# Both product blocks ahead of the fourth projection, and both mask sets ahead of the gates and norms, in the projection rounds of a decoder layer

## The reference

```
q_in = silu(causal_dwconv(x @ Wq, wq_conv))      # k_in, v_in in the same way, 4 taps
q, k = l2norm(q), l2norm(k)                      # per head, 4 heads of 32
v, kb = v * beta[..., None], k * beta[..., None] # beta = sigmoid(x @ Wb)
inv = -(kb @ swap(k)) * strict_lower             # in chunks of 32 tokens, then solved row by row
attn = q @ swap(k) * lower_incl
```

## Time and profile before

| What | us |
|---|---|
| median of 3 runs | 472.37 |
| profiled execution | 472.83 |
| its span | 471.1 |
| busy TensorE, VectorE, ScalarE, GpSimdE | 350.7, 317.4, 152.0, 37.4 |
| the three rounds and the tail | about 31 to 91.5 of the span |

### The profile page before, as it was taken

The page is one execution under the profiler, slowest core; times in us unless marked ns, Lnnn a source line. Parts: engine busy times, 40 slices in busy tenths (PEclk is TensorE's granted clock), DMA queues, the critical chain, the costliest instruction groups (busy, mean ns, idle before and its releaser), DMA issues.

```text
span 471.1 us, 8238 instructions
## 1 busy us (share of the span) xinstructions
PE 350.7 (74%) x2912; PEld 239.2 (51%) x2912; DVE 317.4 (67%) x1049; ACT 152.0 (32%) x267; POOL 37.4 (8%) x74
## 2 busy tenths in 40 slices
PE   3978985968952468343374998979989799878992
PEld 2544553768940456111243556565566555655672
DVE  3046567768999825966536957668876788777535
ACT  1232332223354335222030442224422343314240
POOL 6000000007940000000000000000000000000000
PEclk9999998579966556655567899998999989998997
DMA  7670110299625500000010000000200000000000
GB/s 215 193 196 25 22 22 0 53 287 245 179 69 115 111 4 5 0 1 0 0 46 1 22 1 0 24 0 1 68 1 22 0 0 22 0 1 1 24 1 22
DMA packets 51601, 23.54 MB, mean 50 GB/s; under 512 B 18248, under 2 KB 51056, under 8 KB 51312
## 3 DMA queue, kind: packets, MB, share of 16 engines
q1 hardware_dynamic: 35056, 14.71, 12.5%
q10 hardware_dynamic: 16512, 8.39, 7.0%
HBM read 18.77 MB, written 3.28 MB: 47 GB/s over the span
## 4 chain that ended last, share of the span: by engine, by line
DVE 40%; PE 38%; issue 12%; DMA 4%; ACT 4%; DVEq 1%; SPq 0%; ACTq 0%; POOL 0%
PE bank L484 6%; PE bank L706 5%; PE bank L714 5%; DVE prod L1458 4%; DVE inv L1460 4%; PE bank L459 3%; DVE as_t L1438 3%; DVE nt L1162 3%; DVE nt L1163 3%; PE bank L478 2%; DVE as_t L1260 2%; PE bank L511 2%; DVE as_t L1251 2%; DMA early<-blocks 2%; DVE sm L1164 2%
## 5 line engine op out<-in xcount | busy, mean ns | idle before, releaser
L714 PEld LDWEIGHTS bank<-w_sb,as_t 128*128 128x128 f32 x512 | 61.1, 194 | 22.9 <-issue 18.8
L1018 ACT ACTIVATE as_t<-bank,cb 128x512 f32<-128x512 f32 x64 | 43.3, 686 | 76.1 <-PE bank L706 60.8
L714 PE MATMUL bank<-w_sb,as_t 128*128 128x128 f32 x512 | 63.9, 280 | 5.0 <-ACT as_t L1018 5.0
L706 PE MATMUL bank<-as_t,w_sb 128*128 128x512 f32 x128 | 66.6, 648 | 0.0
L1438 DVE SCALAR_TENSOR_TENSOR as_t<-bank,as_t 128x128 f32<-128x128 f32 x128 | 36.0, 344 | 23.4 <-PE bank L714 21.1
L459 PE MATMUL bank<-ident,as_t 128*128 128x128 f32 (+1 forms) x64 | 12.1, 319 | 33.9 <-DVE as_t L1260 15.7
L484 PE MATMUL bank<-wtap,xc_pad 128*128 128x384 f32 x96 | 35.5, 509 | 0.0
L706 PEld LDWEIGHTS bank<-as_t,w_sb 128*128 128x128 f32 x128 | 24.1, 207 | 20.2 <-issue 18.8
L1229 DVE TENSOR_TENSOR as_t<-bank,masks 128x512 f32 (+1 forms) x32 | 20.0, 686 | 17.2 <-PE bank L511 17.2
L459 PE MATMUL bank<-ident,early 128*128 128x128 f32 x96 | 17.2, 309 | 17.7 <-DVE early L1208 6.0
L459 PEld LDWEIGHTS bank<-ident,as_t 128*128 128x128 f32 (+1 forms) x64 | 7.4, 145 | 42.1 <-DVE as_t L1260 17.3
(11 more groups left out here) (217 smaller groups left out, 614.1 us busy)
## 6 DMA issues: line engine op xcount, KB each, us to landing
toep<-taps_back ACTq DMA_DIRECT2D x8, 1024.0 KB, 8.6
toep<-x SPq DMA_DIRECT2D x8, 256.0 KB, 2.7
early<-x SPq DMA_DIRECT2D x4, 256.0 KB, 3.6
w_sb<-w SPq DMA_DIRECT2D x1, 1024.0 KB
w_sb<-w SPq DMA_DIRECT2D x2, 512.0 KB
blocks<-as_t SPq DMA_DIRECT2D x16, 64.0 KB, 2.0
early<-blocks SPq DMA_DIRECT2D x1, 1024.0 KB, 8.0
src<-vb SPq DMA_DIRECT2D x16, 64.0 KB, 6.5
```

What stands on the lines that cost most here:

```text
L706: pe.matmul(ps[4 + half][:, :], w1_sb[:, e, half * 128:half * 128 + 128], x2_c.rearrange("p b t -> p (b t)"), start=True, stop=True).then_ ...
L714: last = pe.matmul(bank(6 + e % 2)[:, b, :], hid[:, e % 2, half, b * L:(b + 1) * L], w2_sb[:, e, half, :], start=(half == 0), stop=(half = ...
L1018: act.activation(hid[:, e % 2, half, :], ps[4 + half][:, :], ACT.Relu, bias=c_of("b1", 2 * e + half)).then_inc(s["hid_ready"], 1)
```

## The change

In a round TensorE now issues both product blocks before the fourth projection: the order is projection 0, keys, projection 1, block 0, projection 2, block 1, projection 3. It was projection 0, keys, projection 1, projection 2, block 0, projection 3, block 1. VectorE now writes the second mask set directly after the first, before `gate_sums` and `norms`; before, it followed them. No instruction is added, removed or resized, and the tail keeps its code.

```
@@ project_step (TensorE)
                 project(g, 1)
+                products(g - 1, 0)
                 project(g, 2)
-                products(g - 1, 0)
+                products(g - 1, 1)
                 project(g, 3)
-                products(g - 1, 1)
                 if more:
                     x_transposed(g + 1)
@@ the loop over the rounds (VectorE)
                 mask_products(g - 1, 0)
+                mask_products(g - 1, 1)
                 gate_sums(g)
                 norms(g)
-                mask_products(g - 1, 1)
```

## The result

The changed kernel took 475.14 us, the median of six runs (475.02 to 477.15); the kernel before took 471.77 us, the median of six (470.93 to 473.17). The ratio is 1.0083, with a 95% interval of 1.0057 to 1.0108: slower. The forecast was 476.0 us in a range of 474.2 to 477.7.

A forecast was written before the change was run, and what follows sets the result against it. The prediction took a gapless TensorE chain of projections and block 0, then ScalarE's squares and VectorE's reduction, to bound the rounds. Rounds 3.81 + mask waits 0.15 - tail 0.30 = 3.66 us gave 476.0 us, range 474.2 to 477.7.

The forecast's parts named there:

- Block 1 comes onto the chain: Rounds: two blocks instead of one before the fourth projection's end, making it 1.27 us later in each round.
- the term of 3.81 us: Rounds: three rounds at 1.27 us each for block 1 put on TensorE's chain.
- Its split: Cost of a block between projections: 1.08 us its own, 0.19 for the slower start of the projection behind it.
- The wait for the masks: Block 1 needs each bank masked, the fourth just in time: 0.05 us a round, together 0.15.
- The second mask set is covered ahead of the gate sums: VectorE in the rounds: the set fits its idle time with 0.7 us to spare and costs nothing.
- The tail gives back 0.3 us: Tail: without the second mask set there, the first block's matmuls are no longer spread; bounds 0 and 1.21 us.
- The rival of the tail at full clock: Tail: last block meets full clock, about 1.8 us less than forecast, 474.2 us; chance 0.10.
- The rival of the freed stores: Last group's stores part from the load beside them, up to 4.1 us saved, 471.9 us; chance 0.04.
- The sum: Whole kernel: 3.81 + 0.15 - 0.30 = 3.66 us slower, predicted as 476.0 us.

The follow-up runs named there:

- TensorE's half alone: Kernel before with both product blocks ahead of the fourth projection, second mask set still behind the norms; 475.74 us against 472.15, ratio 1.0059.
- block 0 alone: Kernel before with only block 0 moved, from behind the third projection to behind the second; 472.56 us against 472.15, ratio 0.9987.
- The doubled block: Kernel before with block 0 issued twice in a row in each of three rounds, first copy without signal; 474.80 us against 472.15, ratio 1.0075.
- VectorE's half alone: Kernel before with both mask sets ahead of gate sums and norms, TensorE's order unchanged; 479.55 us against 472.15, ratio 1.0130.
- second profile: The changed kernel run once more, with nothing further changed, against the kernel before; 474.87 us against 471.66, ratio 1.0070.

## Why the prediction was right, point by point

- **Block 1 comes onto the chain, 1.27 us a round: shown.** Round 3 is 1.26 us longer (18.00 against 16.74). TensorE's half alone has 1.27 and 1.28 in its two measurable rounds, and block 0 alone has nothing of it. For the third of the three places, in the first round, 1.27 us is assumed and not measured, as the clock differed there. With that the term of 3.81 us stands.
- **Its split was mis-sized.** The prediction took 1.08 us for the block and 0.19 for the change between block and projection. The doubled block shows 0.86 and 0.4. The sum was safe, as it took the two together from one stretch of the chain; anyone who had priced a second block in the same place by 1.27, as one of the experiment's own expectations did, would have been 0.4 us off.
- **The wait for the masks, 0.05 us a round: nothing.** Block 1 starts 3.86 us behind block 0 (57.44 - 53.58), not 3.77, since the projection in front of it now has the slow start too. The last mask ends at 57.35, 0.09 us before it. The prediction took this projection from a row without a block in front.
- **The second mask set is covered ahead of the gate sums: right.** The gate sums wait 0.79 us for ScalarE, as before. That this holds only with block 1 early is shown by VectorE's half alone.
- **The tail gives back 0.3 us: 0.39 (2.50 - 2.11), in both profiles.** The clock was low in the tail as before: a mean of 0.51 from 83.0 to 96.8. The rival of the tail at full clock did not happen.
- **A pause of 0.3 us went: not in the prediction.** It counted nothing that VectorE's new order would give back in the rounds. Without the pause the reductions move by 1.3, 2.2 and 3.5 us in the second profile, not by 1.3, 2.6 and 4.0.
- **The rival of the freed stores fell:** they land in 6.08 us, not 2. But the load behind them came 0.5 to 1.0 us sooner, which the prediction had at nothing.
- **The sum is right in part by luck.** 3.8 - 0.4 - 0.3 (the pause) - 0.5 (the load) is 2.6 us of accounted stages, and the solve starts 2.56 us later in the second profile (4.1 in the first, with the low clock in its first group). The medians differ by 3.4, and the ratio says 3.9 of 471.8, with 2.7 at the low end of its interval. The 0.8 to 1.3 us between are not assigned to a stage. Without them the forecast of 3.66 would have been 1 us too high, mostly because it left out the pause and the load. Single executions of the same kernel differ by 2 us and more.

## What to carry to other kernels

Before moving work of an engine, ask of each piece whether the engine was waiting while it ran. Block 1 stood in TensorE's idle time and cost nothing; the same instructions a few places earlier cost their full length in each round, and the emptier queue behind them was no gain. Price an edit of an order by the distance between two events on the chain, not by the busy time of the operation, because the change between two kinds of work on TensorE costs nearly half as much as a small block here.

## What was not expected of the hardware

- A place where TensorE goes from 128-row projections to the block's 32-row matmuls and back costs about 0.4 us (1.27 for a block between projections, 0.86 for one more beside it). What in the change costs this isn't shown.
- Where TensorE's matmuls waited one by one for VectorE's masks, its granted clock fell from 1.00 to a mean of 0.65 (59.0 to 68.5 us), although it was counted busy for 8.88 of the 9.50 us; the projection behind them took 5.45 us instead of 2.80.
- The same untouched stretch from 26 to 30 us ran at a mean clock of 1.00 in four profiles, at 0.57 or 0.58 in four and at 0.50 in three. In two profiles of the changed kernel (0.50 and 0.57) the first reduction stands at 45.11 and 43.09, which is as much as an edit of this size moves.
